# A fused attention and low-rank-expert layer on eight cores: zero-tile matmuls at the start, weights in quarters over six PSUM banks, and another order of steps in the prologue and slots 0 and 1

## What is computed

```
xn  = layernorm(x)                                  # x is (8, 2048, 1024)
q, k = phi(xn Wq^T), phi(xn Wk^T); v = xn Wv^T      # 8 heads of 64, phi(u) = elu(u) + 1
S_t = g S_(t-1) + k_t v_t^T;  z_t = g z_(t-1) + k_t # per head, g = sigmoid(decay_log)
o_t = (S_t^T q_t) / (z_t . q_t + 1e-6)
attn = (o * sigmoid(xn Wg^T + bg)) Wo^T
s = softmax(x gate_w^T), the two largest of 8 experts
ffn = xn Wlin^T + blin + sum over the two of s_e (xn left_e) right_e   # rank 4
out = x + attn + ffn
```

## Time and profile before

| | |
|---|---|
| device time, median of 3 runs | 262.01 us (261.05 to 262.56) |
| the profiled execution's own time | 263.04 us |
| its span, slowest core (5) | 262.0 us |
| spans of the 8 cores | 258.1 to 262.0 us |
| PE busy | 238.8 us (91%), 1688 matmuls |
| DVE, ACT, POOL busy | 62%, 29%, 24% |
| HBM read, written | 32.00 MB, 8.39 MB |

### The profile page before, as it was taken

The page is one execution under the profiler, slowest core; times in us unless marked ns, Lnnn a source line. Parts: engine busy times, 40 slices in busy tenths (PEclk is TensorE's granted clock), DMA queues, the critical chain, the costliest instruction groups (busy, mean ns, idle before and its releaser), DMA issues.

```text
span 262.0 us, 5276 instructions; the slowest of 8 cores (258.1 to 262.0 us)
## 1 busy us (share of the span) xinstructions
PE 238.8 (91%) x1688; PEld 117.4 (45%) x1688; DVE 162.4 (62%) x425; ACT 76.0 (29%) x128; POOL 61.7 (24%) x99
## 2 busy tenths in 40 slices
PE   0348999999897999999999999999999999999995
PEld 0223454454453555444454555444545454445442
DVE  5365457658857657666566657557566776687522
ACT  2563765576163323312322021111111201000000
POOL 2761100011134230505050402112214030333000
PEclk9999999999999999999999999999999999999999
DMA  6999999999986226352327232233222224343423
GB/s 174 207 175 255 251 169 206 233 181 180 245 219 102 83 60 184 101 155 67 118 78 129 83 101 83 88 94 103 81 100 83 101 83 124 136 140 108 159 104 136
DMA packets 20366, 35.86 MB, mean 137 GB/s; under 512 B 12210, under 2 KB 12530, under 8 KB 20084
## 3 DMA queue, kind: packets, MB, share of 16 engines
q1 hardware_dynamic: 17444, 24.89, 32.9%
q0 software_dynamic: 2896, 10.64, 21.5%
HBM read 32.00 MB, written 8.39 MB: 154 GB/s over the span
## 4 chain that ended last, share of the span: by engine, by line
PE 84%; DVE 6%; DMA 4%; issue 3%; ACT 1%; SPq 0%; DVEq 0%; ACTq 0%
PE PJ L365 26%; PE L L387 17%; PE L L431 9%; PE PJ L358 7%; PE PJ L387 4%; PE L L365 4%; DMA x_sb<-x 4%; PE PJ L431 2%; PE L L358 2%; PE T L336 2%; PE SY L379 2%; PE SY L403 2%; PE T L344 1%; PE T L417 1%; PE SY L407 1%
## 5 line engine op out<-in xcount | busy, mean ns | idle before, releaser
L387 PE MATMUL L<-wlin_sb,xnfm 128*128 128x512 bf16 x208 | 49.2, 379 | 0.0
L323 POOL TENSOR_SCALAR S_blk<-S_sb,small_s 128x260 bf16<-128x260 f32 x30 | 28.6, 969 | 82.7 <-DVE S_sb L814 82.5
L387 PEld LDWEIGHTS L<-wlin_sb,xnfm 128*128 128x128 bf16 x208 | 20.0, 98 | 24.1 <-issue 0.8
L885 ACT ACTIVATE e_sb<-PJ 128x512 bf16<-128x512 f32 x28 | 16.5, 594 | 41.2 <-PE PJ L365 39.7
L643 DVE TENSOR_SCALAR e_sb<-e_sb 128x512 bf16<-128x512 bf16 x32 | 9.7, 303 | 30.0 <-ACT e_sb L885 30.0
L861 ACT ACTIVATE xn_tm<-x_sb,nmr,rstd 128x1024 bf16<-128x1024 f32 x16 | 19.9, 1245 | 25.4 <-POOL nmr L279 23.8
L431 PE MATMUL L<-wo_sb,ygfm 128*128 128x512 bf16 x104 | 26.7, 379 | 0.0
L365 PE MATMUL PJ<-xnfm,wq_sb 128*128 128x512 bf16 x112 | 26.6, 380 | 0.0
L365 PE MATMUL PJ<-xnfm,wg_sb 128*128 128x512 bf16 x112 | 26.6, 379 | 0.0
L365 PE MATMUL PJ<-xnfm,wk_sb 128*128 128x512 bf16 x112 | 26.6, 380 | 0.0
L358 PE MATMUL PJ<-wv_sb,xnfm 128*128 128x512 bf16 x96 | 24.6, 400 | 0.0
(11 more groups left out here) (116 smaller groups left out, 339.0 us busy)
## 6 DMA issues: line engine op xcount, KB each, us to landing
ro_sb<-x SPq DMA_DIRECT2D x16, 512.0 KB, 4.0
out<-ro_sb SPq DMA_DIRECT2D x15, 512.0 KB, 2.7
x_sb<-x SPq DMA_DIRECT2D x10, 512.0 KB, 9.1
x_sb<-x POOLq DMA_DIRECT2D x6, 512.0 KB, 20.5
wlin_sb<-wlin POOLq DMA_DIRECT2D x1, 2048.0 KB, 38.0
wv_sb<-wv POOLq DMA_DIRECT2D x4, 256.0 KB, 11.8
wq_sb<-wq POOLq DMA_DIRECT2D x2, 512.0 KB, 17.6
wk_sb<-wk POOLq DMA_DIRECT2D x2, 512.0 KB, 24.4
```

Source lines behind the costliest of these rows:

```text
L323: GP.tensor_scalar(S_blk[:, :].rearrange("p (q w) -> p q w", q=4)[:, :, 65 * e : 65 * e + 65], S_sb[:, :].rearrange("p (q w) -> p q w", q= ...
L387: TE.matmul(lb(c, n)[:, :], xnk(k, c), wlin_sb[:, D * k + 512 * n : D * k + 512 * n + 512], start=False, stop=False)
L885: SE.activation(e_sb[:, 512 * (n % 2) : 512 * (n % 2) + 512], bank[:, :], AF.Exp).then_inc(ac_e, 1)
```

## The change

1. **Zero tiles.** `warm(n)` issues `n` matmuls of 512 columns of a zeroed `S_blk` into bank SY1, whose content nobody reads: 22 before x0's transposes (they wait only for DVE's zeroing, moved to be its first instruction), 7 between the transposes of x0 and x1, and 4, 2 and 3 within v. They are 38 in all.
2. **Banks and quarters.** `wq`, `wk` and `wg` come in four quarters (6 DMAs more on POOL's queue, x4 to x7 now between them), and v, q, k, gate of block 0 rotate over six banks (`ring6`, with SY0 and SY1). v of chunk 4 stands before k, of 5 before gate, of 6 and `xtr(7)` before gate's last quarter, of 7 behind `tgp(0)`.
3. **DVE's prologue.** Each `xev_v` stands as early as its transposes; `stats(9)` and the router's `top2b(0)` go into slot 0, the latter between the mask products and `phi`.
4. **POOL and ACT.** `rs(9)` and `rs(10)` now stand behind slot 0's `S_blk` and `SG_sb`; `rs(11)` behind slot 1's. `xn(9)` moves into slot 0.
5. **Slots 0 to 2.** `gproj` (gate of the next block) goes ahead of `ytr` in slots 0 and 1. `ktr` writes bank L1 in slots 0 to 2, so that it waits for `ktm_sb` and no longer for `ygfm`; the first `tht` and `threv` use L0, and `right_pair(0)` goes behind `xtr(10)`.

The diff, cut to its core:

```diff
-    ring4 = [PJ[0], PJ[1], L[0], L[1]]
+    KT = [L[1][:, 0:256].bitcast(BF16)] * 3 + [T1[:, 0:512]]
+    TH0 = L[0][:, 0:256].bitcast(BF16)
+    ring6 = [PJ[0], PJ[1], L[0], L[1], SYb[0], SYb[1]]
+    vb = [ring6[i] for i in (0, 1, 2, 3, 2, 0, 5, 2)]
+    qb = [ring6[i] for i in (4, 5, 0, 1)]
+    kb = [ring6[i] for i in (3, 4, 5, 2)]
+    gb = [ring6[i] for i in (3, 4, 0, 1)]
...
+    d_wv, d_wq = [sem(f"d_wv{i}") for i in range(4)], [sem(f"d_wq{i}") for i in range(4)]
+    d_wk, d_wg = [sem(f"d_wk{i}") for i in range(4)], [sem(f"d_wg{i}") for i in range(4)]
+    dv_z = sem("dv_z")
...
+    def wload_q(dst, srcd, i, s):
+        o = 2 * FH * i
+        GP.dma_start(dst[:, o : o + 2 * FH], srcd[:, o : o + 2 * FH]).then_inc(s[i], 16)
...
         for i in range(4):
-            o = 2 * FH * i
-            GP.dma_start(wv_sb[:, o : o + 2 * FH], wv_d[:, o : o + 2 * FH]).then_inc(d_wv[i], 16)
-        wload_half(wq_sb, wq_d, 0, d_wq)
+            wload_q(wv_sb, wv_d, i, d_wv)
+        wload_q(wq_sb, wq_d, 0, d_wq)
+        wload_q(wq_sb, wq_d, 1, d_wq)
         xload(4)
+        wload_q(wq_sb, wq_d, 2, d_wq)
+        wload_q(wq_sb, wq_d, 3, d_wq)
         xload(5)
-        wload_half(wq_sb, wq_d, 1, d_wq)
+        wload_q(wk_sb, wk_d, 0, d_wk)
+        wload_q(wk_sb, wk_d, 1, d_wk)
         xload(6)
+        wload_q(wk_sb, wk_d, 2, d_wk)
+        wload_q(wk_sb, wk_d, 3, d_wk)
         xload(7)
-        wload_half(wk_sb, wk_d, 0, d_wk)
-        wload_half(wk_sb, wk_d, 1, d_wk)
+        wload_q(wg_sb, wg_d, 0, d_wg)
+        wload_q(wg_sb, wg_d, 1, d_wg)
         wload(lg_sb, lg_d, d_lg)
-        wload_half(wg_sb, wg_d, 0, d_wg)
-        wload_half(wg_sb, wg_d, 1, d_wg)
+        wload_q(wg_sb, wg_d, 2, d_wg)
+        wload_q(wg_sb, wg_d, 3, d_wg)
...
         rs(8)
-        rs(9)
         for c in range(NCH):
-            if c + 10 < NCH:
+            if c + 10 < NCH and c >= LAG:
                 rs(c + 10)
...
+            if c == 0:
+                rs(9)
+            if c < LAG:
+                rs(c + 10)
...
+    def warm(n):
+        for _ in range(n):
+            TE.matmul(SYb[1][:, :], S_blk[:, 0:128], S_blk[:, 0:512], start=True, stop=True)
...
+    def gproj(c):
+        TE.wait_ge(dv_k, c + 5)
+        fproj(wg_sb, c // 4 + 1, c % 4, PJ[1], pe_g)
...
+            TE.wait_ge(dv_ktm, 3)
...
     def pe_program():
+        TE.wait_ge(dv_z, 1)
+        warm(22)
         TE.wait_ge(d_id, 16)
         xtr(0)
+        warm(7)
         xtr(1)
         TE.wait_ge(dv_xev, 1)
+        TE.wait_ge(d_wv[0], 16)
+        vproj(0, vb[0], 0, 2)
+        warm(4)
+        TE.wait_ge(dv_xev, 2)
+        vproj(1, vb[1], 0, 2)
+        TE.wait_ge(d_wv[1], 16)
+        for c in range(2):
+            vproj(c, vb[c], 2, 4)
+        warm(2)
         xtr(2)
-        TE.wait_ge(dv_xev, 2)
-        TE.wait_ge(d_wv[0], 16)
-        for c in range(4):
-            if c == 3:
-                xtr(3)
-            TE.wait_ge(dv_xev, c + 1)
-            vproj(c, ring4[c], 0, 2)
-        for i in range(1, 4):
-            TE.wait_ge(d_wv[i], 16)
-            for c in range(4):
-                vproj(c, ring4[c], 2 * i, 2 * i + 2)
-        TE.wait_ge(d_wq[0], 16)
-        for m in range(4):
-            TE.wait_ge(ac_v, m + 1)
-            fproj(wq_sb, 0, m, ring4[m], pe_q, 0, 4)
+        warm(3)
+        TE.wait_ge(d_wv[2], 16)
+        for c in range(2):
+            vproj(c, vb[c], 4, 6)
         TE.wait_ge(dv_xev, 3)
-        xtr(4)
-        TE.wait_ge(d_wq[1], 16)
-        for m in range(4):
-            fproj(wq_sb, 0, m, ring4[m], pe_q, 4, 8)
+        vproj(2, vb[2], 0, 6)
+        xtr(3)
+        TE.wait_ge(d_wv[3], 16)
+        for c in range(3):
+            vproj(c, vb[c], 6, 8)
         TE.wait_ge(dv_xev, 4)
-        xtr(5)
-        for c in (4, 5):
-            TE.wait_ge(dv_xev, c + 1)
-            TE.wait_ge(dv_q, c - 3)
-            vproj(c, ring4[c - 4])
-        TE.wait_ge(d_wk[0], 16)
-        for m in range(4):
-            if m < 2:
-                TE.wait_ge(dv_q, m + 3)
-            else:
-                TE.wait_ge(ac_v, m + 3)
-            fproj(wk_sb, 0, m, ring4[(m + 2) % 4], pe_k, 0, 4)
-        TE.wait_ge(d_wk[1], 16)
-        for m in range(4):
-            fproj(wk_sb, 0, m, ring4[(m + 2) % 4], pe_k, 4, 8)
-        xtr(6)
+        vproj(3, vb[3])
+        for i in range(4):
+            TE.wait_ge(d_wq[i], 16)
+            if i == 3:
+                xtr(4)
+            for m in range(4):
+                if i == 0 and m >= 2:
+                    TE.wait_ge(ac_v, m - 1)
+                fproj(wq_sb, 0, m, qb[m], pe_q, 2 * i, 2 * i + 2)
+        TE.wait_ge(dv_xev, 5)
+        TE.wait_ge(ac_v, 3)
+        vproj(4, vb[4])
+        for i in range(4):
+            TE.wait_ge(d_wk[i], 16)
+            if i == 3:
+                xtr(5)
+            for m in range(4):
+                if i == 0 and m == 0:
+                    TE.wait_ge(ac_v, 4)
+                elif i == 0 and m < 3:
+                    TE.wait_ge(dv_q, m)
+                elif i == 0:
+                    TE.wait_ge(ac_v, 5)
+                fproj(wk_sb, 0, m, kb[m], pe_k, 2 * i, 2 * i + 2)
         TE.wait_ge(dv_xev, 6)
-        xtr(7)
-        TE.wait_ge(d_wg[0], 16)
-        for m in range(4):
-            TE.wait_ge(dv_k, m + 1)
-            fproj(wg_sb, 0, m, ring4[(m + 2) % 4], pe_g, 0, 4)
-        TE.wait_ge(d_wg[1], 16)
-        for m in range(4):
-            fproj(wg_sb, 0, m, ring4[(m + 2) % 4], pe_g, 4, 8)
-        TE.wait_ge(dv_xev, 7)
+        TE.wait_ge(dv_q, 3)
+        vproj(5, vb[5])
+        for i in range(4):
+            TE.wait_ge(d_wg[i], 16)
+            if i == 3:
+                TE.wait_ge(dv_xev, 7)
+                TE.wait_ge(dv_k, 3)
+                vproj(6, vb[6])
+                xtr(7)
+            for m in range(4):
+                if i == 0 and m < 2:
+                    TE.wait_ge(dv_k, m + 1)
+                elif i == 0 and m == 2:
+                    TE.wait_ge(ac_v, 6)
+                elif i == 0:
+                    TE.wait_ge(dv_q, 4)
+                fproj(wg_sb, 0, m, gb[m], pe_g, 2 * i, 2 * i + 2)
+            if i == 1:
+                xtr(6)
         TE.wait_ge(d_lg, 16)
         tgp(0)
-        for c in (6, 7):
-            TE.wait_ge(dv_xev, c + 1)
-            TE.wait_ge(ac_g, c - 5)
-            vproj(c, L[c - 6])
+        TE.wait_ge(dv_xev, 8)
+        TE.wait_ge(dv_k, 4)
+        vproj(7, vb[7])
         for c in range(NCH):
             b, s = c // 4, c % 4
             lo = c - LAG
             more = c < NCH - 4
             TE.wait_ge(dv_k, 4 * b + 4)
             if c == 0:
-                TE.wait_ge(dv_xev, 8)
-            elif c < 4:
+                TE.wait_ge(ac_g, 1)
+            elif c < 3:
+                TE.wait_ge(dv_ktm, c)
+            elif c == 3:
                 TE.wait_ge(dv_gate, c)
             if c < 4:
                 ktr(c)
             if c > 0:
                 TE.wait_ge(dv_norm, c)
+            else:
+                TE.wait_ge(ac_g, 2)
+                TE.wait_ge(ac_v, 7)
             scores(c)
...
-            if lo >= 0:
+            if lo > 0:
                 right_pair(lo)
...
+            if lo == 0:
+                right_pair(0)
             if lo >= 0:
                 lin_group(lo, 0)
             elif more:
@@ -583,7 +634,9 @@
             av(c)
             if c < NCH - 1:
                 TE.wait_ge(dv_ktm, c + 1)
-                if c >= 4:
+                if c == 0:
+                    TE.wait_ge(dv_xev, 8)
+                elif c != 3:
                     TE.wait_ge(dv_gate, c)
                 state(c)
...
-            elif c + 8 < NCH:
+            else:
                 vslot(c)
+                gproj(c)
...
             if s == 0:
-                if c + 8 < XD:
-                    TE.wait_ge(ac_xev, c + 1)
+                if b == 0:
+                    TE.wait_ge(ac_v, 8)
                 tht(b)
             if lo >= 0:
                 o_group(lo, 1)
-            if more:
-                TE.wait_ge(dv_k, c + 5)
-                fproj(wg_sb, b + 1, s, PJ[1], pe_g)
+            if lo >= 0 and more:
+                gproj(c)
...
     def dve_program():
+        VE.memset(S_blk[:, :], 0.0).then_inc(dv_z, 1)
         VE.memset(eps_c[:, :], 1e-5)
         VE.memset(one_c[:, :], 1.0).then_inc(dv_one, 1)
...
         stats(0)
         stats(1)
+        xev_v(0)
         stats(2)
-        xev_v(0)
+        xev_v(1)
         stats(3)
-        xev_v(1)
-        xev_v(2)
-        xev_v(3)
...
+        xev_v(2)
...
+        xev_v(3)
...
         stats(4)
...
         xev_v(4)
...
+        for m in range(4):
+            if m == 2:
+                stats(5)
+            phi(m, qb[m], fm(qfm, 0)[:, 512 * m : 512 * m + 512], dv_q)
+        stats(6)
         xev_v(5)
...
+        for m in range(4):
+            phi(4 + m, kb[m], fm(kfm, 0)[:, 512 * m : 512 * m + 512], dv_k)
         stats(7)
-        VE.wait_ge(ac_mk, 1)
+        xev_v(6)
```

(33 more changed lines are left out.)

56 lines of the change are left out of this document (15 added, 41 removed).

## The result

The changed kernel takes **265.14 us** (median; 264.64 to 265.69) against 262.12 for the kernel before on the same chip: ratio 1.0122, 95% interval 1.0085 to 1.0159. The forecast was 260.2 with 257.5 to 263.2, so it missed by 4.9 us, and on the wrong side of no change. The profiled execution took 265.28 us.

What follows compares the result with a forecast made beforehand. PE was taken as the bound: 56.3 to slot 0, 22.7 for slots 0 and 1 and 178.9 after make 257.9; with 2.3 for the slow clock, 260.2 in span, and 260.2 as median. Range 257.5 to 263.2.

Steps and rivals of the forecast that it cites:

- v starts: Prologue: v's matmuls start at 16.1 us, when wv's first quarter lands, where they started at 17.55.
- v, with the clock's loss: Prologue, v's start to q: ends at 25.9 at full clock, against 29.62 (-3.7 us); the slow clock takes back 2.3.
- second part: Prologue from q's start to slot 0: 30.4 us with six banks, 30.9 before, -0.5.
- slots 0 and 1: From slot 0's start to slot 2: 22.7 us, 22.6 before, +0.1, with two PE waits of 2.0 in slot 1.
- slot 2 to the end: From slot 2 to the kernel's end: unchanged, 178.9 us.
- span: Whole kernel on the slowest core: 257.9 us at full clock, 260.2 with the clock's loss, against 262.0 before.
- its gain of 1.8: Whole kernel: the gain applied to both span and median, making both 260.2 us.
- The wait is in two halves: Slot 1: argument against a clock fall there, as 4.0 of 4.5 us idle are split into two waits of 2.0.
- that rival: The clock falls in slot 1 as well as at the start: +2.6 us, 262.8; chance 0.21.
- give them back in one place: Slots 0 and 1: the two rs behind SG_sb return the old waits that the gate and ktr moves remove; +0.1 us.
- The 9 tiles in v: Prologue, within v: the zero tiles cost 1.9 us, counted in full since no wait is left for them to fill.
- The six DMAs at nothing: Weight loads: six more DMAs cost nothing; upper bound 8.2 us, with late quarters as a rival at 261.7, chance 0.04.

Runs made afterwards that it cites:

- e13: Changed kernel with zero tiles in slot 1's two waits, 9 ahead of x9's transposes and 14 behind, their operand last in SBUF; 262.99 us, ratio 1.0043.
- e1: Changed kernel without any of its 38 zero tiles; 263.69 us, ratio 1.0055 to the kernel before.
- e12: Changed kernel with POOL waiting for x10's load before it issues wlin; 265.27 us, ratio 1.0142 to the kernel before.
- e15: Changed kernel with 14 zero tiles added behind x1's transposes and none within v, slots left as they are; 262.60 us, ratio 1.0041.
- e5: Changed kernel with only the tanh of gate moved directly behind v's eviction on ACT in slots 0 and 1; 261.88 us, ratio 0.9978.
- e6: Changed kernel with x9's statistics, rs(9) and xn(9) ahead of slot 0, rs(10) and rs(11) ahead of S_blk, tanh still last; 261.99 us, ratio 0.9986.
- e4: Changed kernel with the order changes of both e5 and e6; 259.24 us, ratio 0.9882 to the kernel before.
- e11: e9 without the 9 zero tiles within v; 256.50 us, ratio 0.9794 to the kernel before.
- e10: e7 with wq, wk and wg loaded in halves, six DMAs fewer; 257.94 us, ratio 0.9844 to the kernel before.
- e8: e4 without any zero tile; 259.68 us, ratio 0.9905 to the kernel before.
- e9: e7 with POOL waiting for x10's load before it issues wlin; 257.24 us, ratio 0.9824 to the kernel before.
- e7: e4 with 14 more zero tiles behind x1's transposes, in the wait for wv; 260.45 us, ratio 0.9922 to the kernel before.

## Why the prediction was wrong

The sum against core 0 of the profiled execution:

| step | forecast | measured | off by |
|---|---|---|---|
| v starts | 16.1 | 16.29 | +0.2 |
| v, with the clock's loss | 9.8 + 2.3 | 12.64 | +0.5 |
| second part | 30.4 | 30.80 | +0.4 |
| slots 0 and 1 | 22.7 | 24.90 | +2.2 |
| slot 2 to the end | 178.9 | 179.57 | +0.7 |
| span | 260.2 | 264.2 | +4.0 |

The last 0.9 is the step from the span to the median: the forecast took its gain of 1.8 off the median, while the profiled execution before was 1.0 above that median and the one after was at it.

**Slots 0 and 1 are the step that failed.** The walk through the engines' orders was nearly right: waits of 2.0 and 2.0 at the places named, behind the `rs` that stand behind `SG_sb`, and the tanh last; measured 2.47 and 1.91. What the forecast priced at nothing was the clock behind them. "The wait is in two halves" was the argument against that rival (0.21, 262.8). The clock fell on all eight cores all the same, and e13 puts its cost at about 2 us. The rival's mechanism was right. The 5.2 us of slow clock behind its price of 2.6 rested on no row, and the price was, if anything, high; its time came out too low because the rest of the sum, start, waits, the part from slot 2 and the median, was short by 2.9. With the cluster filled (e13) the median is 262.99, inside the stated range and 2.8 above the forecast.

The Trainium skill (TensorE: Matmul & The Clock Gate, Why this matters for your kernels), by which the clock drops on a single long idle gap, was read in the forecast as saying that two waits of 2.0 with transposes between them would pass. The runs decide otherwise: two of 2.47 and 1.91 brought the clock down on all eight cores, and on all eight again in e1, e12 and e15, where they stayed. Even a single wait did so on three of eight cores in e5, while one of 3.43 in e6 did not.

**The verdict on the clog should have come from the order alone.** The forecast wrote that the two `rs` "give them back in one place" and booked +0.1. e6 shows that without them slots 0 and 1 take 21.0 where x10 is in time, and e4 that they could take 19.5. A part of the change that takes back all of another part's gain is a weak place, not a neutral one: 4.4 us of idle time in one slot are the first candidate for whatever depends on idle time.

**Slot 2 to the end** was taken over unchanged. A wait of 0.5 for `S_sb` ahead of slot 2's `ytr` was not in the walk, which stopped at slot 2. It stands on seven cores of the changed kernel and on none in e4, e5 and e6. But e1, which has the cluster, shows it on one core only, and e13, where the clock held, on all eight; what brings it stays open.

**The start** was right in kind: zero tiles raise the clock, it is lost in the wait for `wv`, v starts slowly. But the gain was counted against core 5, the latest of eight in one execution. In the mean q started at 27.1 before and 27.3 after: no gain at all, and slot 0 followed 31.1 later against 31.2 before, so six banks and quarters brought 0.1. The forecasts of v's start and of q on the slowest core (27 to 29, measured 28.93) came true, but the 29.62 that the gain was taken from was the chance of one execution. The 9 tiles in v were booked at 1.9; taking them out brought q 1.2 forward (e11), and they buy nothing. Which core is slow in the start differs from run to run, and the slowest of eight decides.

**The six DMAs at nothing** held for the changed kernel, but for core 5, where PE waited 0.87 and 0.71 for quarters of `wk`. `wg` was whole at 46.5 to 48.8 (51.8 on core 5) against 45.5 to 46.5 before. e10 shows 1.6 us for six. The 2 us per DMA that the Trainium skill gives (DMA: Bandwidth & Descriptors, Anatomy of one DMA) would be 12 for them if paid one after another, an estimate; the runs show nothing like it.

What stays open: why the same wait of 2.45 us kept the clock on one core of e5 and lost it on the next (and 3.43 kept it in e6 where 1.85 lost it in e8), and, for want of an experiment, which part of slot 1's 2 us each of the two waits would have cost alone. At the start core 6 alone kept its clock; its wait for `wv` was the shortest, 1.62, and 2.02 on core 3 lost it.

## What to carry to other kernels

Where a walk through the orders gathers small waits of a busy PE into one place, price the clock behind them as a cost of its own, here about 2 us behind 4.4 us of waits; a wait that nothing else can fill is the place for zero tiles, and running matmuls are not. Read a start that depends on the clock on all cores, and count its gain against their mean as well as against the slowest. Before a stage is shortened, look for the transfer that is due next: x10, landing with 2 MB of `wlin`, held slots 0 and 1 at up to 23.8 us, until one wait on POOL put it first and they took 19.5 on every core.

## What the runs showed of the hardware

- Two waits of 2.47 and 1.91 with a group of transposes between them brought the granted clock down on all eight cores (0.72 to 0.86 from 70 to 82 us). One wait of about 2.5 us in slot 1 left it at 1.00 on five cores and brought it down on three (e5). Length alone does not decide: 3.43 kept it (e6, core 4), 3.72 (e6, core 2) and 1.85 (e8, core 1) lost it.
- At the start the granted clock can read 1.00 where the pace is half: so on core 5 before the change from 12 to 26 us, with four matmuls at 1.87.
- Matmuls on zeros raise the clock as others do: transposes at 10 us take 0.61 and not 1.01, and with 14 more in the wait the clock reads 1.00 from 16 to 22 us on all eight cores of e9, where v's first two matmuls take 0.59 (1.01 at half clock on core 0 of the changed kernel).
- A 512 KB load issued behind a 2 MB one on another queue landed with it: x10 at 65.6, `wlin` at 65.5 (changed kernel, core 0), and x10 at 51.8 to 54.9 when `wlin` is issued only after it has landed (e9).
- Six DMAs more for the same bytes: packets of the software queue 2896 to 3760, the last part of `wg` landing 1.6 us later in the mean (e7 against e10).
